# A new order of the attention step, Q and K through the score banks, and 24 leading products on PE

## The chip, the cores and the metric

The kernel runs on one core of a Trainium2 chip. The metric is device time in microseconds (us) of one execution, less is better. The kernel before takes 1670.7 us, the median of 3 runs (1669.65 to 1671.39).

## What is computed

128 sequences of 128 tokens with 256 features: a cross-attention with 16 heads, an additive bias for every head, query and key, and low-rank additions to the three projections, then a layernorm and a mixture of 8 experts in which each token goes to one.

```python
def attention(q, ctx, bias):               # q = layernorm(x); lora(z, W, b, A, B) = z W^T + b + 2 (z A^T) B^T
    qh, kh, vh = lora(q, "q"), lora(ctx, "k"), lora(ctx, "v")        # 16 heads of 16
    scores = einsum('bqhd,bkhd->bhqk', qh * 16 ** -0.5, kh) + bias   # bias: [128, 16, 128, 128] f32
    return einsum('bhqk,bkhd->bqhd', softmax(scores), vh)

x = x + tanh(g_xattn) * attention(layernorm(x), ctx, bias)
idx = argmax(softmax(z @ Wg + bg)) ; z = layernorm(x)
x = x + tanh(g_ffn) * (gelu(z @ W1[idx] + b1[idx]) @ W2[idx] + b2[idx])
```

## The kernel before, in words

Each of the five engines has its own program; semaphores join them and every engine keeps strictly to the order that is written. There are three stages: a setup (weights loaded by 21 transfers, low-rank products L432 to L436, small DVE work), the attention loop, and the expert stage with 72 tiles of 256 tokens. The change touches the first two.

The attention loop is a software pipeline by hand (`run_steps`, L87). Step k works on several sequences at once; `seq(i, k, lag)` names sequence k - lag. A `cur` (lag 0) sequence gets its scores in this step; `prev` (lag 1) is transposed and exponentiated; `fin` (lag 2) is multiplied by V and normalised; `old` (lag 3) has its second layernorm; `gate` (lag 4) gets its expert logits; `nxt` (lag -4) is prepared.

In one step of the kernel before PE does, in this order: `scores` (L451, all four score banks `b_s[0..3]`), the transposes `turn` 0 and 1 (L464), the product with V called PV here (L490, into bank `b_x`), the transposes of the second normalised row block (L502, into `b_x2`, which is `b_s[1]`), the transposes of the attention output OT (L515), logits (L519) and, in every fourth step, slot positions (L523, L524), all three into `b_o`, then the transposes of the next x and ctx (L536, L539, into `b_x`), `turn` 2 and 3, the V projection (L551, L553, into `b_v`, which is `b_s[0]`), and alternately the Q projection (L559) or the K projection (L569) for a pair of sequences, both into `b_x`.

ACT does `probs` (L658, exponentials of a turned quarter), two `normalise` (L651), and the copies out of PSUM: OT (L674), x2T (L679), XT (L687), V (L695), QT (L631), KT (L642).

DVE adds the bias to each score quarter (`add_bias`, L778, four per step, frees a score bank by `s_used`), takes row maxima (L784), then waits for `o_ready` and works on the output bank: L863, L867, L871, L878, with the statistics of the coming layernorms (L792, L795, L801) and at the end L893, which makes `ve`. POOL takes `ve` to the power -1/2 into `rs` (L396), after its two `subtract_max` (L380). DVE makes `shift` from `rs` (L850) one step later, and ACT's `normalise` needs `shift`. In every fourth step DVE begins with `pick_experts` (L806 to L822), in the step behind it with `list_slots`.

Of the kernel before, what the change touches and what calls it, by code (L numbers as in the profile page):

```python
# [98 lines left out]
def flamingo_block(nc, x, ctx_in, bias, g_xattn, g_ffn, wqT, bq, aq, bqT, wkT, bk, ak, bkT, wvT, bv, av, bvT,  # L99
                   wg, bg, w1, w2, b2, consts, row_consts, ids_const, out):  # L100
    ctx = ExitStack()
    with ctx:
# [3 lines left out]
        def sem(name):  # L106
            return ctx.enter_context(nc.semaphore(name))
# [87 lines left out]
        b_v, b_x2 = b_s[0], b_s[1]  # L195
# [5 lines left out]
        s_set = sem("s_set")  # L201
# [33 lines left out]
        SETUP_DMAS = 21  # L235
        SETUP_OPS = 15
# [192 lines left out]
        def _(pe):  # L429
            mm = nc.tensor.matmul  # L430
            pe.wait_ge(s_set, 16 * SETUP_DMAS)
# [34 lines left out]

            def step(i, k):
                nxt, late, cur, prev, fin, old, gate = (seq(i, k, lag) for lag in (-4, -2, 0, 1, 2, 3, 4))
                was_nxt, was_late, was_gate, was_grp = (seq(i, k, lag) for lag in (-3, -1, 5, 6))
                if cur:  # L470
                    pe.wait_ge(v_evac, nxt.n() if nxt else N)
                    if gate:
                        pe.wait_ge(x2t_evac, gate.n(1, 1))
                    scores(cur)
                if prev:
                    turn(prev, 0)
                    turn(prev, 1)

                if was_nxt and was_nxt.slot(2) == 1:
                    pe.wait_ge(q_evac, was_nxt.per(2, 1, 1))  # L480
                if was_late and was_late.slot(2) == 0:
                    pe.wait_ge(k_evac, was_late.per(2, 1, 1))
                if fin:
                    pe.wait_ge(pt_ready, fin.n(4, 4))
                    if fin.reached(1):
                        pe.wait_ge(ot_evac, fin.n())
                    pe.wait_ge(xt_evac, nxt.n() if nxt else N)
                    for h in range(HEADS):
                        j = h % 4
                        ins = mm(b_x[CELL * j:CELL * j + CELL, P * (h // 4):P * (h // 4) + P],  # L490
                                 V[:, fin.slot(8), h, :], PT[:, fin.slot(2), P * h:P * h + P],
                                 start=True, stop=True, tile_position=(0, CELL * j))
                    ins.then_inc(ot_ready, 1)
                if old:
                    pe.wait_ge(xn2_ok, old.n(1, 1))
                    if cur:
                        pe.wait_ge(s_used, cur.n(4, 2))
                    else:
                        pe.wait_ge(s_used, 4 * N)
                        pe.wait_ge(x2t_evac, old.n())  # L500
                    for c in range(KC):
                        ins = nc.tensor.transpose(b_x2[:, c * P:c * P + P],  # L502
                                                  xn2[:, old.slot(8), c * P:c * P + P], ident)
                    ins.then_inc(x2t_ready, 1)

                ins = None
                grp = seq(i, k, 5)
                if old:
                    pe.wait_ge(x2_ok, old.n())
                elif was_gate:  # L510
                    pe.wait_ge(l_ok, was_gate.n(1, 1))
# [13 lines left out]
                if ins:  # L525
                    ins.then_inc(o_ready, 1)
                if nxt:
                    pair, tok = nxt.k // 2 % 2, P * nxt.slot(2)
                    pe.wait_ge(xn_ok, nxt.n(1, 1))
                    pe.wait_ge(ctx_inn[nxt.slot(4)], nxt.per(4, 16, 16))  # L530
                    if nxt.reached(1):
                        pe.wait_ge(xt_evac, nxt.n())
                    if fin:
                        pe.wait_ge(ot_evac, fin.n(1, 1))
                    for c in range(KC):
                        nc.tensor.transpose(b_x[:, c * P:c * P + P],  # L536
                                            xn[:, nxt.slot(2), c * P:c * P + P], ident)
                    for c in range(KC):
                        ins = nc.tensor.transpose(b_x[:, (KC + c) * P:(KC + c) * P + P],  # L539
                                                  ctx_sb[:, nxt.slot(4), c * P:c * P + P], ident)  # L540
                    ins.then_inc(xt_ready, 1)
                if prev:
                    turn(prev, 2)
                    turn(prev, 3)
                if nxt:
                    pe.wait_ge(xt_evac, nxt.n(1, 1))
                    if cur:
                        pe.wait_ge(s_used, cur.n(4, 1))
                    elif nxt.reached(1):
                        pe.wait_ge(v_evac, nxt.n())  # L550
                    mm(b_v[:, 0:HID], top3[:], bv_rows[:], start=True, stop=False)  # L551
                    for c in range(KC):
                        ins = mm(b_v[:, 0:HID], XT[:, pair, KC + c, tok:tok + P], W["v"][:, c, :],  # L553
                                 start=False, stop=(c == KC - 1))
                    ins.then_inc(v_ready, 1)
                if nxt and nxt.slot(2) == 1:
                    for o in range(KC):
                        for c in range(KC):
                            ins = mm(b_x[:, 256 * o:256 * o + 256], W["q"][:, c, o * P:o * P + P],  # L559
                                     XT[:, pair, c, :], start=(c == 0), stop=(c == KC - 1))  # L560
                    ins.then_inc(q_ready, 1)
                if late and late.slot(2) == 0:
                    pair = late.k // 2 % 2
                    pe.wait_ge(xt_evac, nxt.n(1, 1) if nxt else N)
                    if fin:
                        pe.wait_ge(ot_evac, fin.n(1, 1))
                    for o in range(KC):
                        for c in range(KC):
                            ins = mm(b_x[:, 256 * o:256 * o + 256], W["k"][:, c, o * P:o * P + P],  # L569
                                     XT[:, pair, KC + c, :], start=(c == 0), stop=(c == KC - 1))  # L570
                    ins.then_inc(k_ready, 1)
# [47 lines left out]
        def _(act):  # L619
# [5 lines left out]
            def queries(t):  # L625
                pair = t.k // 2 % 2
                act.wait_ge(q_ready, t.per(2, 1, 1))
                if t.reached(4):
                    act.wait_ge(s_ready, t.n(4, -8))
                for o in range(KC):  # L630
                    ins = nc.scalar.activation(QT[:, pair, o, :], b_x[:, 256 * o:256 * o + 256],  # L631
                                               ACT.Identity, bias=bq_col[:, o:o + 1])
                ins.then_inc(q_evac, 1)

            def keys(t):
                pair = t.k // 2 % 2
                act.wait_ge(k_ready, t.per(2, 1, 1))
                if t.reached(4):
                    act.wait_ge(s_ready, t.n(4, -8))
                for o in range(KC):  # L640
                    for e in range(2):
                        ins = nc.scalar.activation(  # L642
                            KT[:, pair, o, :, e, :], b_x[:, 256 * o:256 * o + 256].rearrange("p (s k) -> p s k", s=2),
                            ACT.Identity, bias=bk_half[:, e, o:o + 1], scale=half_rows[e])
# [16 lines left out]
            def step(i, k):  # L661
                nxt, late, prev, fin, old = (seq(i, k, lag) for lag in (-4, -2, 1, 2, 3))
                if prev:
                    probs(prev, 0)
                    probs(prev, 1)
# [4 lines left out]
                if fin:  # L670
# [3 lines left out]
                    nc.scalar.copy(OT[:], b_x[:]).then_inc(ot_evac, 1)  # L674
                if old:
# [5 lines left out]
                if nxt:  # L681
                    pair, tok = nxt.k // 2 % 2, P * nxt.slot(2)
                    act.wait_ge(xt_ready, nxt.n(1, 1))
                    if nxt.reached(4):
                        act.wait_ge(q_ready, nxt.per(2, 1, -1))
                        act.wait_ge(k_ready, nxt.per(2, 1, -1))
                    nc.scalar.copy(XT[:, pair, :, tok:tok + P],  # L687
                                   b_x[:].rearrange("p (c t) -> p c t", t=P)).then_inc(xt_evac, 1)
                if prev:
                    probs(prev, 2)  # L690
                if nxt:
                    act.wait_ge(v_ready, nxt.n(1, 1))
                    if nxt.reached(8):
                        act.wait_ge(ot_ready, nxt.n(1, -7))
                    nc.scalar.copy(V[:, nxt.slot(8), :, 0:D],  # L695
                                   b_v[:, 0:HID].rearrange("p (h d) -> p h d", d=D)).then_inc(v_evac, 1)
                if prev:
                    probs(prev, 3)
                if nxt and nxt.slot(2) == 1:
                    queries(nxt.minus(1))  # L700
                if late and late.slot(2) == 0:
                    keys(late)
# [25 lines left out]
        def _(dve):  # L728

# [106 lines left out]
            def step(i, k):  # L836
# [7 lines left out]
                if cur:  # L844
                    add_bias(cur, 0)
# [6 lines left out]
                if cur:  # L852
                    add_bias(cur, 1)
# [162 lines left out]
```

## Time and profile before

| what | value |
|---|---|
| median of 3 runs | 1670.7 us |
| time of the profiled execution | 1668.51 us |
| its span, first to last instruction | 1666.6 us |
| PE, busy share of the span | 87% |
| DVE | 64% |
| POOL | 57% |
| ACT | 53% |
| mean share of the 16 DMA engines (hardware and software queue) | 61% |
| first scores / end of the attention stage / span | 57.7 / about 1300 / 1666.6 us |

The times of the rows are microseconds from the start of the span. In a timeline row the first number is the start, the second the duration of a group of like instructions that follow each other, "x8" their number, and the bracket says how long the engine was idle before them and what ended that.

### The profile page before, as it was taken

The numbers are of one execution on the slowest core, as the hardware profiler recorded it, in microseconds if no ns is written. First come the engines' busy times: TensorE is split into PE (matmuls) and PEld (weight loads), VectorE is DVE, ScalarE is ACT, GpSimd is POOL, SyncE is SP. The second block draws the span as 40 slices with busy tenths as digits, with TensorE's granted clock in tenths as the row PEclk, the third lists the DMA queues.
The fourth block names the chain that finished last, engine by engine and source line by source line (L and its number), as shares of the span: only waits on it lengthen the run. The fifth ranks groups of instructions, "written<-read, shape, count | busy, mean of one in ns | idle before, by whom it ended". The sixth has DMA issues, their size and how long they took to land.

```text
span 1666.6 us, 43159 instructions
## 1 busy us (share of the span) xinstructions
PE 1450.7 (87%) x13374; PEld 1166.7 (70%) x13374; DVE 1061.8 (64%) x2734; ACT 887.9 (53%) x1883; POOL 942.9 (57%) x671
## 2 busy tenths in 40 slices
PE   3789999989989989989998998998997589999886
PEld 2577777777777777777777777777776468777775
DVE  2477787787788788778778778778877311111111
ACT  1466666666666666666666666666664123333231
POOL 2345555555555555556555555555555356666667
PEclk9999999999999999999999999999999699999998
DMA  4355655555555555555555555555552499999994
GB/s 140 85 164 150 178 163 154 171 170 153 166 175 152 163 174 156 160 175 157 157 174 163 157 168 168 155 167 171 154 166 66 139 249 253 242 226 229 230 221 93
DMA packets 383026, 281.53 MB, mean 169 GB/s; under 512 B 21599, under 2 KB 349691, under 8 KB 382972
## 3 DMA queue, kind: packets, MB, share of 16 engines
q1 hardware_dynamic: 356092, 246.22, 50.8%
q0 software_dynamic: 26880, 34.64, 10.5%
q8 instruction: 29, 0.48, 0.1%
q14 instruction: 25, 0.20, 0.0%
HBM read 226.86 MB, written 56.00 MB: 170 GB/s over the span
## 4 chain that ended last, share of the span: by engine, by line
PE 51%; ACT 18%; DMA 15%; issue 10%; DVE 2%; SPq 1%; POOL 1%; ACTq 1%; POOLq 0%; DVEq 0%
DMA out<-og,ids 14%; PE bank L464 9%; PE bank L553 7%; PE bank L569 7%; PE bank L559 7%; ACT KT L642 5%; PE bank L515 5%; PE bank L451 4%; ACT OT L674 4%; ACT x2n L651 3%; ACT xn L651 3%; PE bank L519 3%; ACT PT L658 2%; PE bank L536 2%; PE bank L598 2%
## 5 line engine op out<-in xcount | busy, mean ns | idle before, releaser
L380 POOL TENSOR_TENSOR sc<-sc,negmax 128x1024 f32<-128x1024 f32 x256 | 484.4, 1892 | 435.6 <-DVE negmax L784 435.6
L778 DVE TENSOR_TENSOR sc<-bank,sc 128x512 f32<-128x512 f32 x512 | 337.6, 684 | 195.2 <-PE bank L451 192.4
L658 ACT ACTIVATE PT<-bank 128x512 f32<-128x512 f32 x512 | 293.3, 603 | 59.7 <-PE bank L464 59.7
L784 DVE TENSOR_REDUCE negmax<-sc 128x8 f32<-128x1024 f32 x256 | 312.3, 1220 | 17.0
L420 POOL DMA_INDIRECT out<-og,ids x144 | 223.5, 1552 | 132.3 <-issue 112.0
L464 PE MATMUL bank<-cst,sc 128*128 128x128 f32 x2048 | 273.6, 277 | 0.7 <-ACT PT L658 0.7
L464 PEld LDWEIGHTS bank<-cst,sc 128*128 128x128 f32 x2048 | 226.6, 142 | 43.1 <-issue 41.8
L943 DVE TENSOR_SCALAR og<-bank,tg 128x512 f32<-128x512 f32 x72 | 54.0, 750 | 276.1 <-DMA out<-og,ids 240.5
L687 ACT COPY XT<-bank 128x512 f32<-128x512 f32 x128 | 75.0, 586 | 183.8 <-PE bank L539 183.8
L396 POOL TENSOR_TENSOR rs<-ve,cst 128x2 f32<-128x2 f32 (+1 forms) x135 | 94.8, 703 | 119.4 <-DVE ve L893 98.9
L642 ACT ACTIVATE KT<-bank,bk_half,cst 128x256 f32<-128x256 f32 x256 | 123.7, 564 | 56.5 <-PE bank L569 56.5
L405 POOL DMA_INDIRECT rows_dram<-x2n,slot_i x128 | 133.5, 1043 | 33.2 <-issue 28.9
L451 PE MATMUL bank<-KT,QT 32*128 32x256 f32 x2048 | 146.7, 400 | 0.0
L612 PE MATMUL bank<-sc,hT 128*128 128x256 f32 x576 | 144.4, 380 | 0.0
L598 PE MATMUL bank<-xgT,w_sb 128*128 128x256 f32 x576 | 140.0, 387 | 4.5 <-issue 2.8
L490 PE MATMUL bank<-PT,V 128*32 128x128 f32 x4096 | 139.2, 277 | 0.7 <-ACT PT L658 0.7
L515 PE MATMUL bank<-cst,OT 128*128 128x128 f32 x512 | 82.4, 284 | 64.1 <-ACT OT L674 63.6
L553 PE MATMUL bank<-wv,XT 128*128 128x256 f32 x512 | 134.6, 386 | 0.0
L712 ACT COPY xgT<-bank 128x512 f32<-128x512 f32 x72 | 42.2, 586 | 158.0 <-PE bank L587 158.0
L451 PEld LDWEIGHTS bank<-KT,QT 32*128 32x128 f32 x2048 | 92.5, 184 | 45.0 <-issue 42.2
L559 PE MATMUL bank<-XT,wq 128*128 128x256 f32 x512 | 123.0, 384 | 0.0
L569 PE MATMUL bank<-XT,wk 128*128 128x256 f32 x512 | 122.4, 382 | 0.0
(120 smaller groups left out, 2196.7 us busy)
## 6 DMA issues: line engine op xcount, KB each, us to landing
sc<-in_bias SPq DMA_DIRECT2D x256, 512.0 KB, 5.1
xg<-rows_dram SPq DMA_DIRECT2D x72, 272.0 KB, 4.0
w_sb<-in_w SPq DMA_DIRECT2D x72, 257.0 KB, 4.1
sc<-in_w SPq DMA_DIRECT2D x72, 256.0 KB
ctx_sb<-in_ctx_in SPq DMA_DIRECT2D x128, 128.0 KB, 5.3
x_sb<-in_x SPq DMA_DIRECT2D x128, 128.0 KB, 2.1
out<-x SPq DMA_DIRECT2D x128, 128.0 KB, 1.7
rows_dram<-vacant SPq DMA_DIRECT2D x9, 272.0 KB, 3.6
```

Source lines behind the costliest of these rows:

```text
L380: nc.gpsimd.tensor_tensor(s, s, m, ALU.add).then_inc(sub_ok, 1)
L420: nc.gpsimd.indirect_dma_start(out_rows, bass.IndirectOffsetOnAxis(ap=ids[:, t.slot(8), a:a + 1], axis=0), og[:, t.slot(2), a, :], None, b ...
L451: ins = mm(b_s[j][:, 2 * P * c:2 * P * c + 2 * P], QT[rows, pair, c, P * sq:P * sq + P], KT[rows, pair, c, sq].rearrange("p e k -> p (e k) ...
L464: ins = nc.tensor.transpose(b_t[q % 2][:, P * h:P * h + P], sc[:, t.slot(4), o:o + P], ident)
L553: ins = mm(b_v[:, 0:HID], XT[:, pair, KC + c, tok:tok + P], W["v"][:, c, :], start=False, stop=(c == KC - 1))
L559: ins = mm(b_x[:, 256 * o:256 * o + 256], W["q"][:, c, o * P:o * P + P], XT[:, pair, c, :], start=(c == 0), stop=(c == KC - 1))
L569: ins = mm(b_x[:, 256 * o:256 * o + 256], W["k"][:, c, o * P:o * P + P], XT[:, pair, KC + c, :], start=(c == 0), stop=(c == KC - 1))
L598: ins = mm(bank[2 + t.slot(2)][:, FT * o:FT * o + FT], w1_sb[:, t.slot(4), c * HID + o * P:c * HID + o * P + P], xgT[:, t.slot(2), c, :], ...
L642: ins = nc.scalar.activation(KT[:, pair, o, :, e, :], b_x[:, 256 * o:256 * o + 256].rearrange("p (s k) -> p s k", s=2), ACT.Identity, bias ...
L658: nc.scalar.activation(PT[:, t.slot(2), 512 * q:512 * q + 512], b_t[q % 2][:], ACT.Exp).then_inc(pt_ready, 1)
L778: nc.vector.tensor_tensor(s, b_s[q][:], s, ALU.add).then_inc(s_used, 1)
L784: nc.vector.tensor_reduce(negmax[:, t.slot(2), 8 * h:8 * h + 8], sc[:, t.slot(4), 1024 * h:1024 * h + 1024].rearrange("p (h k) -> p h k", ...
```

## The change

The PE, ACT and DVE programs of the attention step are put in another order, Q and K get their own lags and other banks, and PE's program starts with 24 products.

- PE: scores, PV, turn 0 and 1, then Q (sequence k+2, even steps) or K (sequence k+1, odd steps) into `b_s[0]` and `b_s[1]` behind a wait for two add_bias of this step, turn 2 and 3, OT, logits and positions, V of the sequence of lag -3 into `b_s[2]`, the x2n transposes into `b_s[3]`, and last the x and ctx transposes of `nxt`.
- ACT: both `normalise`, OT, probs 0 and 1, QT or KT (each half as soon as its own product is there), probs 2 and 3, V, x2T, XT.
- DVE: `shift` (L850) stands ahead of the first `add_bias`.
- Setup: DVE clears `xgT`, and PE multiplies a 128x128 part of it by itself 24 times ahead of its wait for the weights.

```diff
-        b_v, b_x2 = b_s[0], b_s[1]
+        b_v, b_x2 = b_s[2], b_s[3]
+            pe.wait_ge(s_warm, 1)
+            for n in range(WARM):
+                mm(bank[7][:, 0:P], xgT[:, 0, 0, 0:P], xgT[:, 0, 0, 0:P], start=True, stop=True)
             pe.wait_ge(s_set, 16 * SETUP_DMAS)
...
+            def project(w, t, first, ready):
+                pe.wait_ge(xt_evac, t.n(1, 2))
+                for o in range(KC):
+                    for c in range(KC):
+                        ins = mm(b_s[o][:, 0:2 * P], W[w][:, c, o * P:o * P + P],
+                                 XT[:, t.k // 2 % 2, first + c, :], start=(c == 0), stop=(c == KC - 1))
+                    ins.then_inc(ready, 1)
...
+                if prev:
+                    turn(prev, 0)
+                    turn(prev, 1)
+                if cur and (qry or ky):
+                    pe.wait_ge(s_used, cur.n(4, 2))
+                if qry and qry.slot(2) == 0:
+                    if qry.reached(2):
+                        pe.wait_ge(k_evac, qry.per(2))
+                    project("q", qry, 0, q_ready)
+                if ky and ky.slot(2) == 0:
+                    pe.wait_ge(q_evac, ky.per(2, 1, 1))
+                    project("k", ky, KC, k_ready)
+                if prev:
+                    turn(prev, 2)
+                    turn(prev, 3)
...
+                if val:
+                    pair, tok = val.k // 2 % 2, P * val.slot(2)
+                    pe.wait_ge(xt_evac, val.n(1, 1))
+                    if cur:
+                        pe.wait_ge(s_used, cur.n(4, 3))
...
+                if old:
+                    pe.wait_ge(xn2_ok, old.n(1, 1))
+                    if cur:
+                        pe.wait_ge(s_used, cur.n(4, 4))
...
-                if cur:
-                    add_bias(cur, 0)
                 norms = norms_at(i, k - 1)
                 if norms:
                     a, b = norms
...
                 if cur:
+                    add_bias(cur, 0)
                     add_bias(cur, 1)
```

## Rows read from the trace of the kernel before

**Rows 1.** The stages view: busy us of each engine, steps 6 to 123.
```profile
108.96:1237.75 1128.79, 1025.44 (x10764) 825.32 (x10763) 894.47 (x2307) 712.85 (x1520) 644.24 (x464) 1.00 0.56 164
```
**Rows 2.** The timeline of PE: the scores of sequences 0, 4 and 124.
```profile
57.73 1.15 PE L451 MATMUL bank<-KT,QT 32*128 32x256 f32 x16
...
89.97 1.15 PE L451 MATMUL bank<-KT,QT 32*128 32x256 f32 x16
...
1247.33 1.15 PE L451 MATMUL bank<-KT,QT 32*128 32x256 f32 x16
```
**Rows 3.** The timeline of PE, one step.
```profile
842.42 1.15 PE L451 MATMUL bank<-KT,QT 32*128 32x256 f32 x16
...
844.52 1.08 PE L490 MATMUL bank<-PT,V 128*32 128x128 f32 x32
845.89 0.43 PE L502 MATMUL bank<-cst,x2n 128*128 128x128 f32 x2 [0.29 <-ACT x2n L651]
846.77 0.66 PE L515 MATMUL bank<-cst,OT 128*128 128x128 f32 x4 [0.45 <-ACT OT L674]
847.27 0.51 PE L519 MATMUL bank<-wg_sb,x2T 128*128 128x8 f32 x4
847.63 0.42 PE L536 MATMUL bank<-cst,xn 128*128 128x128 f32 x2
...
848.10 1.04 PE L464 MATMUL bank<-cst,sc 128*128 128x128 f32 x8
...
850.00 1.89 PE L569 MATMUL bank<-XT,wk 128*128 128x256 f32 x8
851.82 1.15 PE L451 MATMUL bank<-KT,QT 32*128 32x256 f32 x16
```
**Rows 4.** The waits view of steps 6 to 123: total, times, longest us.
```profile
DVE sc L778 <- PE bank L451: 168.9, 105, 2.2
...
DVE lmax L806 <- issue: 4.1, 12, 0.4
```
**Rows 5.** The timeline of DVE in the same step.
```profile
843.58 0.69 DVE L778 TENSOR_TENSOR sc<-bank,sc 128x512 f32<-128x512 f32 x1 [2.24 <-PE bank L451]
...
848.65 0.16 DVE L863 TENSOR_TENSOR L<-bank,bg_all 128x8 f32<-128x8 f32 x1
...
850.89 0.17 DVE L893 TENSOR_SCALAR ve<-mv 128x2 f32<-128x2 f32 x1
```
**Rows 6.** The timeline of POOL, same step: the power behind L893.
```profile
851.14 0.72 POOL L396 TENSOR_TENSOR rs<-ve,cst 128x2 f32<-128x2 f32 x1 [0.43 <-DVE ve L893]
```
**Rows 7.** The timeline of DVE, a step that begins with pick_experts.
```profile
860.37 0.18 DVE L806 TENSOR_REDUCE lmax<-L 128x4 f32<-128x32 f32 x1
...
862.62 0.69 DVE L778 TENSOR_TENSOR sc<-bank,sc 128x512 f32<-128x512 f32 x1 [0.21 <-PE bank L451]
```
**Rows 8.** The timeline of PE, the positions of such a step and what follows.
```profile
828.02 0.39 PE L523 MATMUL bank<-OH,cst 128*128 128x32 f32 x2
...
828.47 0.42 PE L536 MATMUL bank<-cst,xn 128*128 128x128 f32 x2
```
**Rows 9.** The timeline of ACT, the copy of x2T.
```profile
846.61 0.39 ACT L679 COPY x2T<-bank 128x256 f32<-128x256 f32 x1
```
**Rows 10.** The timeline ahead of the first scores.
```profile
11.51 2.07 PE L434 MATMUL bank<-bq,aq 8*128 8x256 f32 x4 [11.51 <-DMA cnt<-in_bg]
...
34.51 0.60 ACT L651 ACTIVATE xn<-x_sb,shift,rs 128x256 f32<-128x256 f32 x1
...
38.85 3.62 PE L559 MATMUL bank<-XT,wq 128*128 128x256 f32 x8
```
**Rows 11.** The stages view, 10 to 20 us (columns as in rows 1).
```profile
10.00:20.00 10.00, 5.48 (x12) 3.82 (x12) 2.75 (x10) 0.20 (x1) 0.00 (x0) 1.00 0.01 0
```
**Rows 12.** The timeline of DVE: the first bias addition of sequences 126 and 127.
```profile
1263.63 0.69 DVE L778 TENSOR_TENSOR sc<-bank,sc 128x512 f32<-128x512 f32 x1
...
1270.87 0.69 DVE L778 TENSOR_TENSOR sc<-bank,sc 128x512 f32<-128x512 f32 x1
```

More of the change, by code:

```diff
@@ L198, in flamingo_block @@
         pos_ps = o_ps[:, 1:HEADS:4, D + 4:D + 4 + EXPERTS]
-        s_set = sem("s_set")
+        s_set, s_warm = sem("s_set"), sem("s_warm")
         s_bv, bv_in, s_b2, b2_out = sem("s_bv"), sem("bv_in"), sem("s_b2"), sem("b2_out")
@@ L235, in flamingo_block @@
         SETUP_DMAS = 21
+        WARM = 24
         SETUP_OPS = 15
@@ L465, in turn @@
                 ins.then_inc(tr_ready, 1)
+            def project(w, t, first, ready):
[5 more added lines that the diff above has]
+                    ins.then_inc(ready, 1)
             def step(i, k):
-                nxt, late, cur, prev, fin, old, gate = (seq(i, k, lag) for lag in (-4, -2, 0, 1, 2, 3, 4))
-                was_nxt, was_late, was_gate, was_grp = (seq(i, k, lag) for lag in (-3, -1, 5, 6))
+                nxt, val, qry, ky, cur, prev, fin, old, gate, grp = (
+                    seq(i, k, lag) for lag in (-4, -3, -2, -1, 0, 1, 2, 3, 4, 5))
+                was_gate = seq(i, k, 5)
                 if cur:
-                    pe.wait_ge(v_evac, nxt.n() if nxt else N)
+                    pe.wait_ge(v_evac, val.n() if val else N)
                     if gate:
@@ L474, in step @@
                     scores(cur)
[L475 to L482, printed above, removed]
                 if fin:
                     pe.wait_ge(pt_ready, fin.n(4, 4))
-                    if fin.reached(1):
-                        pe.wait_ge(ot_evac, fin.n())
                     pe.wait_ge(xt_evac, nxt.n() if nxt else N)
@@ L493, in step @@
                     ins.then_inc(ot_ready, 1)
-                if old:
-                    pe.wait_ge(xn2_ok, old.n(1, 1))
-                    if cur:
[L497 to L509, printed above, removed]
+                if prev:
[13 more added lines that the diff above has]
+                    turn(prev, 3)
+                ins = None
+                if old:
+                    pe.wait_ge(x2_ok, old.n(1, 1))
                 elif was_gate:
@@ L526, in step @@
                     ins.then_inc(o_ready, 1)
+                if val:
[3 more added lines that the diff above has]
+                        pe.wait_ge(s_used, cur.n(4, 3))
+                    elif val.reached(1):
+                        pe.wait_ge(v_evac, val.n())
+                    mm(b_v[:, 0:HID], top3[:], bv_rows[:], start=True, stop=False)
+                    for c in range(KC):
+                        ins = mm(b_v[:, 0:HID], XT[:, pair, KC + c, tok:tok + P], W["v"][:, c, :],
+                                 start=False, stop=(c == KC - 1))
+                    ins.then_inc(v_ready, 1)
+                if old:
+                    pe.wait_ge(xn2_ok, old.n(1, 1))
+                    if cur:
+                        pe.wait_ge(s_used, cur.n(4, 4))
+                    else:
+                        pe.wait_ge(s_used, 4 * N)
+                        pe.wait_ge(x2t_evac, old.n())
+                    for c in range(KC):
+                        ins = nc.tensor.transpose(b_x2[:, c * P:c * P + P],
+                                                  xn2[:, old.slot(8), c * P:c * P + P], ident)
+                    ins.then_inc(x2t_ready, 1)
                 if nxt:
-                    pair, tok = nxt.k // 2 % 2, P * nxt.slot(2)
                     pe.wait_ge(xn_ok, nxt.n(1, 1))
@@ L541, in step @@
                     ins.then_inc(xt_ready, 1)
[L542 to L571, printed above, removed]
             run_steps(pe, FIRST, LAST, U, LOOP, step)
@@ L626, in queries @@
                 pair = t.k // 2 % 2
-                act.wait_ge(q_ready, t.per(2, 1, 1))
                 if t.reached(4):
@@ L630, in queries @@
                 for o in range(KC):
-                    ins = nc.scalar.activation(QT[:, pair, o, :], b_x[:, 256 * o:256 * o + 256],
+                    act.wait_ge(q_ready, t.per(2, KC, o + 1))
+                    ins = nc.scalar.activation(QT[:, pair, o, :], b_s[o][:, 0:2 * P],
                                                ACT.Identity, bias=bq_col[:, o:o + 1])
@@ L636, in keys @@
                 pair = t.k // 2 % 2
-                act.wait_ge(k_ready, t.per(2, 1, 1))
                 if t.reached(4):
@@ L640, in keys @@
                 for o in range(KC):
+                    act.wait_ge(k_ready, t.per(2, KC, o + 1))
                     for e in range(2):
                         ins = nc.scalar.activation(
-                            KT[:, pair, o, :, e, :], b_x[:, 256 * o:256 * o + 256].rearrange("p (s k) -> p s k", s=2),
+                            KT[:, pair, o, :, e, :], b_s[o][:, 0:2 * P].rearrange("p (s k) -> p s k", s=2),
                             ACT.Identity, bias=bk_half[:, e, o:o + 1], scale=half_rows[e])
@@ L661, in step @@
             def step(i, k):
[L662 to L665, printed above, removed]
+                nxt, val, qry, ky, prev, fin, old = (seq(i, k, lag) for lag in (-4, -3, -2, -1, 1, 2, 3))
                 if old:
@@ L674, in step @@
                     nc.scalar.copy(OT[:], b_x[:]).then_inc(ot_evac, 1)
+                if prev:
+                    probs(prev, 0)
+                    probs(prev, 1)
+                if qry and qry.slot(2) == 0:
+                    queries(qry)
+                if ky and ky.slot(2) == 0:
+                    keys(ky)
+                if prev:
+                    probs(prev, 2)
+                    probs(prev, 3)
+                if val:
+                    act.wait_ge(v_ready, val.n(1, 1))
+                    if val.reached(8):
+                        act.wait_ge(ot_ready, val.n(1, -7))
+                    nc.scalar.copy(V[:, val.slot(8), :, 0:D],
+                                   b_v[:, 0:HID].rearrange("p (h d) -> p h d", d=D)).then_inc(v_evac, 1)
                 if old:
@@ L684, in step @@
                     if nxt.reached(4):
-                        act.wait_ge(q_ready, nxt.per(2, 1, -1))
-                        act.wait_ge(k_ready, nxt.per(2, 1, -1))
+                        act.wait_ge(k_ready, nxt.per(2, KC, -KC))
                     nc.scalar.copy(XT[:, pair, :, tok:tok + P],
                                    b_x[:].rearrange("p (c t) -> p c t", t=P)).then_inc(xt_evac, 1)
[L689 to L702, printed above, removed]
             run_steps(act, FIRST, LAST, U, LOOP, step)
@@ L728, in _ @@
         def _(dve):
+            nc.vector.memset(xgT[:], 0.0).then_inc(s_warm, 1)
             dve.wait_ge(s_set, 16 * SETUP_DMAS)
@@ L843, in step @@
                     list_slots(was_grp)
-                if cur:
-                    add_bias(cur, 0)
                 norms = norms_at(i, k - 1)
```

## Prediction

> **What bounds the kernel now.** I read the stages view first: from step 6 to step 123 PE is busy 1025 of 1129 us, DVE 894, ACT 713, POOL 644, the DMA engines 56%, at full granted clock [rows 1]. PE is the fullest, so the next view is its timeline. The starts of the scores give the length of a step: from sequence 4 to 124 it is (1247.33 - 89.97) / 120 = 9.645 us [rows 2]. Inside one step PE stands twice, 0.29 us for the second normalised block and 0.45 us for OT [rows 3]; both are ACT copies whose input PE made a moment before. By starts, which leave out the overlap, the work of a step is: scores with turn 0 and 1 2.10, PV about 1.05 (its 1.08), L502 0.23 (half of four transposes, 0.47), L515 0.50 and L519 0.36, x and ctx 0.47, turn 2 and 3 with V 1.90, K 1.82 [rows 3]. That is 8.43 us of 9.40; the rest, 0.97 us, is the two waits with the draining that goes with them. DVE meanwhile waits 168.9 us in those 117 steps for scores, 1.44 us a step [rows 4]. So PE's order bounds the loop, and DVE follows by a little over a microsecond.
>
> **PE's part.** No product is added or removed in the loop. What moves: PV goes ahead of the turns, so ACT copies OT under 0.9 us of turns, 1.74 us of Q or K and 0.9 us of turns; that wait goes (0.45 us). The x2n transposes stand near the end of the step, and `normalise` for them at its head, several us earlier; that wait goes too (0.29 us). What is late next on PE is the border of two steps: the next scores need x2T copied. L502 takes 0.43 us [rows 3], the copy 0.39 [rows 9], handovers some 0.1 together (an estimate from those rows), so scores can start 0.92 us after L502 starts, while PE has only 0.23 + 0.47 us to do there, and some 0.08 for the change of tiling: a gap of about 0.14 us. PE alone would therefore need 8.43 + 0.14 = 8.57 us, less about 0.1 since three changes of tiling stand in the order in place of four: 8.5, and the pick step 0.45 more for positions [rows 8]. That would be 8.6 us a step.
>
> The trace shows no scores directly followed by PV. The nearest rows are scores followed by turns and turns followed by PV; I bound the pair between 0.1 us less and 0.35 us more than the sum above. The Trainium skill, TensorEngine Tiling (Array Packing), Key Properties, says that changing the tiling mode drains TensorE; by that rule alone the new order has one drain less, which would be a gain of about 0.1 us a step and no loss. The sum holds without it.
>
> **DVE's part, which I take for the new bound.** DVE is strictly in order, and `shift` now stands ahead of the first add. It waits for POOL's `rs`, which waits for DVE's last operation of the step before. Queued behind that wait are all four adds, both maxima and the output work; PE's Q or K waits for the second add, and all of PE's step stands behind that. The loop, from add to add [rows 5]: add to L863 is 5.07 us, less 0.07 for the shift that leaves it, 5.00; L863 to L893 2.24; from L893 to POOL's start 0.25 and 0.72 for the power [rows 6]; then 0.05 and 0.08 until the add. Together 8.34 us, against 9.40 now, where the same wait was hidden under the wait for scores.
>
> L863 waits for `o_ready` on PE. Two adds (2 x 0.69, less overlap, 1.33 [rows 5]) free the banks; then Q or K 1.74, turns 0.91, L515 0.50 and L519 until its end 0.51 make 3.66 [rows 3], plus handovers 0.05: 5.04 us after the add. DVE itself is there after 5.00. So both chains run side by side with 0.04 us between: DVE-PE-DVE. In the pick step, once in four, pick_experts takes from 860.37 to 862.62, and the add was hardly waiting for PE there [rows 7]; it stands in line with `shift` behind L893, 2.40 us in all against 1.10 for the round trip of `rs`: +1.30. Positions add 0.45 to `o_ready` in that step [rows 8], with the 0.04 above. list_slots and the extra operation cost between 0 (hidden behind `rs`) and 0.5 us; I take 0.25, an estimate. At the head of each loop of 8 steps 0.34 us is lost (4.1 / 12 [rows 4]), 0.04 a step. Four steps: 4 x 8.34 + 1.30 + 0.25 + 3 x 0.04 + 0.49 = 35.5, or 8.88 a step, and 0.04: **8.92 us**. That is above PE's 8.6, so PE will stand for some 0.3 us a step, in the pick step over a microsecond ahead of Q or K. 120 steps x (9.645 - 8.92) = **87 us** less.
>
> ACT has the room: 713 us in 117 steps is 6.1 us a step [rows 1]. Its QT or KT work is hidden behind turns, OT and V, and costs up to 1 us a step if it comes late. POOL's 5.5 us are hidden too. On SP nothing is moved; the transfers run at 56% [rows 1] and would go to 61%; the output store and what is queued behind it on SP wait for x2, about 0.8 us later in a step, hidden by a bias that is loaded three steps ahead.
>
> **The ends of the loop.** Ahead of the first scores, steps are a single chain: the second xn starts at 34.51 because ACT first copied V [rows 10], and Q takes 3.62 us in line with the rest. The new order lets xn, the transposes and XT of one sequence run while V, Q or K of an earlier one is on PE. Going through the four steps by these durations I get the first scores at 44.5 to 47.5 us, against 57.73 [rows 2]; I take 12 us less. The four short steps behind it give 1 us. At the end, the last three adds followed DVE's own work at once (7.24 us from 126 to 127, no wait [rows 12]); there the round trip of `rs`, about 0.9 us, is now exposed three times, plus a little in the drain: +3 us.
>
> **The 24 products.** PE waits until 11.51 us for the weights; then 12 passes of 256 columns take 5.48 us busy [rows 10, 11]. Passes of Q stand 0.43 us apart at 38.85 (3.62 for 8) [rows 10], those of K 0.23 (1.82 for 8) [rows 3]. 
>
> **Sum:** 87 + 12 + 1 + 2 - 3 = 99 us. Against the profiled execution: 1668.5 - 99 = 1569.5; the median of the runs lies 2.2 us above that execution, so about 1572 us. The expert stage is not touched.
>
> **The rivals.**
> - *PE is still the bound.* Were `rs` back sooner, or the order tighter than I read it, the step would be PE's 8.6: 120 x 1.045 + 12 = 137 less, **1533 us**. For it: PE is the fullest engine [rows 1]. Against it: the round trip [rows 5, 6] contains no slack. 7%.
> - *PE and DVE couple worse than the sum.* Drains between scores and PV, late KT copies, or `s_used` arriving late each go once through the loop DVE-PE-DVE, where only 0.04 us is free. Price 0.2 to 0.5 us a step, 24 to 60 us: **1596 to 1632 us**. For it: the 0.04. Against it: all terms are from rows at full clock. 23%.
> - *The moved `shift` makes it slower.* The wait for `rs` comes ahead of the first add and PE's Q or K waits behind it; if that wait were longer than the PE work between scores and Q or K (2 us) by more than the 0.73 us that the order gains, all gain is gone. The 1.10 us round trip would have to be 1.8 us or more in every step, for instance because POOL reaches L396 late behind its two L380: 2 us a step instead gives 9.85 a step, 120 x 0.2 = 24 slower, less 12: **1683 us**. Against it: POOL waited for `ve`, not `ve` for POOL [rows 6]. 4%.
> - *The reordering hides nothing* because an ACT copy takes the place of those removed, 0.7 us at the border in place of 0.14: about 9.6 us a step, only the head of the loop gains, **1658 us**. 3%.
>
> **How the numbers follow.** My forecast has 63%: its own bounds are 8.8 to 9.1 us a step and 8 to 13 us at the head, 1555 to 1598. The range that holds 8 in 10 takes in half of the first rival and most of the second: 1545 to 1616. A measurement of this kernel can tell about 0.2% (3.3 us) from no change. Faster 0.95, same 0.01, slower 0.04.
>
> **What would show it.** In the profile of the changed kernel: scores 8.9 us apart, with every fourth step about 1.5 us longer; DVE idle ahead of `shift` with POOL's `rs` as releaser, and hardly any wait for scores; PE idle ahead of Q or K with the second add as releaser; no wait ahead of L515's and L502's successors; first scores near 45 us; the low-rank products at 0.23 us a pass. I am wrong if PE waits longest at the border of steps, if DVE still waits for scores, or if the first scores are later than 50 us.

## The result and the profile after

The changed kernel takes **1594.9 us** (median of 4, 1591.2 to 1599.0) against 1670.2, a ratio of 0.9558 (95% interval 0.9518 to 0.9599): 4.4% faster. The forecast was 1572 (1545 to 1616). The gain is 75 us where 99 were forecast. One term of the sum, 2 us for the 24 products, was mis-sized by much more: without them the kernel took 21 to 120 us longer, which only an experiment showed.

The profiled execution took 1598.95 us, its span is 1596.9. The timeline of PE, the scores of sequences 0, 4 and 124 (to be read against [rows 2]):

```profile
43.94 1.15 PE L455 MATMUL bank<-KT,QT 32*128 32x256 f32 x16
...
74.90 1.15 PE L455 MATMUL bank<-KT,QT 32*128 32x256 f32 x16
...
1166.66 1.15 PE L455 MATMUL bank<-KT,QT 32*128 32x256 f32 x16
```

The first scores come 13.8 us sooner, the four short steps behind them give 1.3, and 120 steps of (1166.66 - 74.90) / 120 = 9.098 us in place of 9.645 give 65.6. From the scores of sequence 124 to the first expert tile it is 5.9 us more than before (74.17 against 68.27), and the untouched expert stage behind it is 5.1 us longer in this execution (356.1 against 351.0; in a second profile of the changed kernel it is 350.8). 13.8 + 1.3 + 65.6 - 5.9 - 5.1 = 69.7, the difference of the two spans.

The waits view from 200 to 1100 us (total, times, longest us) shows the new bound. These are the waits of DVE and PE that bear on it; ACT and POOL wait longer in total, behind DVE and PE:

```profile
DVE shift L844 <- POOL rs L397: 53.1, 74, 0.9
...
PE bank L475 <- DVE sc L774: 39.2, 41, 2.0
...
DVE L L858 <- PE bank L530: 13.2, 24, 2.1
...
DVE x L873 <- issue: 4.9, 10, 0.8
```

The wait of DVE for scores, 168.9 us before [rows 4], is not in the list any more (in the same window of the kernel before it was 131.3). DVE now stands ahead of `shift` for POOL's `rs`, PE stands ahead of Q or K for the second bias addition, and DVE for the positions of the pick step. One step of it, in the timelines of DVE, POOL and PE:

```profile
638.26 0.17 DVE L888 TENSOR_SCALAR ve<-mv 128x2 f32<-128x2 f32 x1
...
639.34 0.16 DVE L844 SCALAR_TENSOR_TENSOR shift<-mv,rs 128x2 f32<-128x2 f32 x1 [0.91 <-POOL rs L397]
639.44 1.29 DVE L774 TENSOR_TENSOR sc<-bank,sc 128x512 f32<-128x512 f32 x2
```
```profile
638.59 0.72 POOL L397 TENSOR_TENSOR rs<-ve,cst 128x2 f32<-128x2 f32 x1 [0.80 <-DVE ve L888]
```
```profile
637.74 1.15 PE L455 MATMUL bank<-KT,QT 32*128 32x256 f32 x16
638.82 1.08 PE L493 MATMUL bank<-PT,V 128*32 128x128 f32 x32
639.83 1.09 PE L468 MATMUL bank<-cst,sc 128*128 128x128 f32 x8
640.78 1.99 PE L475 MATMUL bank<-XT,wq 128*128 128x256 f32 x8
...
646.21 1.15 PE L455 MATMUL bank<-KT,QT 32*128 32x256 f32 x16
```

The two additions end at 640.73 and Q starts at 640.78. The turns in front of it ended their issue at about the same time: in such a step (8.47 us) both chains arrive together. In the pick step they don't:

```profile
619.18 0.19 DVE L802 TENSOR_REDUCE lmax<-L 128x4 f32<-128x32 f32 x1 [0.34 <-issue]
...
621.55 1.29 DVE L774 TENSOR_TENSOR sc<-bank,sc 128x512 f32<-128x512 f32 x2
```
```profile
622.90 1.99 PE L475 MATMUL bank<-XT,wq 128*128 128x256 f32 x8 [1.33 <-DVE sc L774]
```

The DVE timeline from 100 to 1160 us, taken apart as in the prediction and averaged over 29 groups of four steps (us; in brackets what was forecast, where 2.57 is the 2.40 of the pick step and half of the 0.34 us that is lost once in 8 steps at the head of a round):

| step, from its first addition | add to L858 | L858 to ve | ve to next add | sum |
|---|---|---|---|---|
| behind pick_experts | 5.61 (5.49) | 2.43 (2.49) | 1.20 (1.10) | 9.25 (9.08) |
| the next | 5.17 (5.04) | 2.27 (2.24) | 1.17 (1.10) | 8.61 (8.38) |
| the next | 5.03 (5.04) | 2.32 (2.24) | 1.13 (1.10) | 8.48 (8.38) |
| the one that ends with pick_experts | 5.17 (5.04) | 2.43 (2.24) | 2.58 (2.57) | 10.18 (9.85) |

The 5.61 is 5.50 in 27 of 29 steps and 7.17 in the two in which PE's clock had fallen (see the last section).

### The profile page after: what moved, and what is told of

Its sections match the earlier page's. It is cut to its first block, busy times and chain, and to the rows that moved or that the text cites. A ratio compares the mean times of both kernels' runs of the same rounds, so it can differ in the third digit from the quotient of the medians.

```text
span 1596.9 us, 43185 instructions
## 1 busy us (share of the span) xinstructions
PE 1431.2 (90%) x13422; PEld 1194.2 (75%) x13422; DVE 1077.9 (68%) x2735; ACT 899.5 (56%) x1883; POOL 942.8 (59%) x671
## 4 chain that ended last, share of the span: by engine, by line
PE 36%; DMA 25%; DVE 16%; issue 12%; POOL 6%; SPq 3%; DVEq 1%; POOLq 0%; ACT 0%; ACTq 0%
DMA out<-og,ids 16%; PE bank L475 10%; DMA rows_dram<-x2n,slot_i 8%; PE bank L468 8%; POOL sc L381 4%; PE bank L455 3%; DVE sc L774 3%; PE bank L493 3%; PE bank L542 3%; PE bank L521 2%; PE bank L525 2%; DVE st L791 2%; DVE x L873 2%; DVE CNT L818 1%; DVE mv L797 1%
## 5 line engine op out<-in xcount | busy, mean ns | idle before, releaser
L774 DVE TENSOR_TENSOR sc<-bank,sc 128x512 f32<-128x512 f32 x512 | 328.5, 683 | 3.8 <-PE bank L455 2.5
L656 ACT ACTIVATE PT<-bank 128x512 f32<-128x512 f32 x512 | 277.9, 597 | 2.9 <-PE bank L468 2.9
L468 PEld LDWEIGHTS bank<-cst,sc 128*128 128x128 f32 x2048 | 231.7, 142 | 46.2 <-issue 32.7
L649 ACT ACTIVATE x2n<-x,shift,rs 128x256 f32<-128x256 f32 x128 | 76.9, 601 | 226.7 <-DVE shift L844 193.1
L475 PE MATMUL bank<-XT,wq 128*128 128x256 f32 x512 | 130.3, 398 | 41.7 <-DVE sc L774 41.0
L475 PEld LDWEIGHTS bank<-XT,wq 128*128 128x128 f32 x512 | 93.5, 193 | 63.0 <-DVE sc L774 49.1
L493 PEld LDWEIGHTS bank<-PT,V 128*32 128x32 f32 x4096 | 104.6, 110 | 42.4 <-issue 42.3
L475 PE MATMUL bank<-XT,wk 128*128 128x256 f32 x512 | 125.6, 388 | 11.2 <-DVE sc L774 8.4
L455 PEld LDWEIGHTS bank<-KT,QT 32*128 32x128 f32 x2048 | 98.4, 184 | 47.8 <-ACT V L684 38.3
```

Source lines behind the costliest of these rows:

```text
L455: ins = mm(b_s[j][:, 2 * P * c:2 * P * c + 2 * P], QT[rows, pair, c, P * sq:P * sq + P], KT[rows, pair, c, sq].rearrange("p e k -> p (e k) ...
L468: ins = nc.tensor.transpose(b_t[q % 2][:, P * h:P * h + P], sc[:, t.slot(4), o:o + P], ident)
L475: ins = mm(b_s[o][:, 0:2 * P], W[w][:, c, o * P:o * P + P], XT[:, t.k // 2 % 2, first + c, :], start=(c == 0), stop=(c == KC - 1))
L656: nc.scalar.activation(PT[:, t.slot(2), 512 * q:512 * q + 512], b_t[q % 2][:], ACT.Exp).then_inc(pt_ready, 1)
L774: nc.vector.tensor_tensor(s, b_s[q][:], s, ALU.add).then_inc(s_used, 1)
```

## The experiments

The theories: **A**, DVE with the round trip of `rs` sets the step, closely followed by PE (A'); **B**, PE alone; **C**, the scatter of x2n rows holds DVE up at the x2 addition, which explains the gaps in the third column of the table. All times are medians. Differences are taken from the 1592.0 us of the changed kernel's second timing; it stood beside the first four runs, while the others stood beside the kernel before alone, and their ratios to that one are given.

**The changed kernel again.**

> The changed kernel itself, as the yardstick for the other runs beside it: 1592 to 1599 us, scores 9.1 us apart, against 1670 for the kernel before.

1592.0 us (1590.5 to 1593.7), ratio 0.9545 (0.9519 to 0.9571), 9.103 us a step.

**The round trip made longer.**

```diff
+ nc.gpsimd.tensor_tensor(spare[:, a:b, 0], ve[:, a:b, 0], minus_half.broadcast_to([P, b - a]), ALU.pow)
  nc.gpsimd.tensor_tensor(rs[:, a:b, 0], ve[:, a:b, 0], minus_half.broadcast_to([P, b - a]), ALU.pow).then_inc(rs_ok, 1)
```

> The changed kernel with one more power of the same size on POOL ahead of the one that makes rs, 0.72 us; nothing reads its result. Theory A (the round trip of rs stands in the loop DVE-POOL-DVE-PE): three steps of four are longer by about 0.7 us, the one that pick_experts hides is not, so 0.5 us a step and 60 to 65 us in all, about 1657 us. Theory B (PE alone bounds the step now, and DVE has slack): under 10 us.

1652.3 us, 60 more. The timelines of POOL and DVE:

```profile
640.47 0.72 POOL L398 TENSOR_TENSOR spare<-ve,cst 128x2 f32<-128x2 f32 x1 [0.56 <-DVE ve L891]
641.17 0.68 POOL L400 TENSOR_TENSOR rs<-ve,cst 128x2 f32<-128x2 f32 x1
```
```profile
641.88 0.16 DVE L847 SCALAR_TENSOR_TENSOR shift<-mv,rs 128x2 f32<-128x2 f32 x1 [1.57 <-POOL rs L400]
```

By kind of step, add to add: 9.79, 9.26, 9.12 and 10.13. The three steps that wait for `rs` are 0.54 to 0.66 us longer than in the table, the one that pick_experts covers is not longer. That is A, and B, PE alone, falls.

**The scatter's wait on another engine.**

```diff
 # DVE, ahead of the x2 addition
-dve.wait_ge(x2_out[done.slot(8)], done.per(8, 16))
 # ACT, ahead of normalise of x2, one step later
+if old.reached(8):
+    act.wait_ge(x2_out[old.slot(8)], old.per(8, 16))
```

> The changed kernel, but the wait for the scatter of x2n rows (x2_out) stands on ACT ahead of normalise one step later, no longer on DVE ahead of the x2 addition. Theory C (the scatter, which is issued one step before and takes 5.7 us to land, holds DVE up by 0.067 us a step on average, over 0.2 us in a dozen steps): 5 to 10 us less, and no gap over 0.61 us ahead of the x2 addition. Rival (those gaps are hidden by PE anyway): within 2 us.

1580.8 us, 11 less, ratio 0.9473 (0.9444 to 0.9503), 9.01 us a step; L858 to ve falls to 2.39, 2.25, 2.25 and 2.25 us. C holds, a little above its range. Inside the loop of the changed kernel (100 to 1160 us) the scatter takes 4.2 to 6.7 us to land (median 5.7); it is issued behind `rs` of one step, and the x2 addition of the next now comes some 6.1 us later, where before it came 7.1. So only the slow landings are late, and DVE stood ahead of 28 of 116 such additions. One of those gaps, in a pick step of the changed kernel:

```profile
910.35 0.42 DVE L873 TENSOR_TENSOR x<-bank,x_sb 128x256 f32<-128x256 f32 x1 [0.59 <-issue]
```

**shift behind the first addition again.**

```diff
+if cur: add_bias(cur, 0)
 if norms: ... shift ...
-if cur: add_bias(cur, 0)
```

> The changed kernel with shift behind the first bias addition again, all else as changed. Theory A in its strict form (DVE with the round trip alone sets the time): 0.6 us of the round trip is hidden in three steps of four, 0.45 us a step, 54 us less, about 1541. Theory A' (DVE's loop of 8.4 us and PE's own work of 8.4 us stand side by side, so taking one away leaves the other): 0.1 to 0.2 us a step, 12 to 25 us less, 1570 to 1583. If moving shift ahead was what made the order work: slower.

1573.9 us, 18 less, ratio 0.944 (0.9415 to 0.9464): A', not the strict form. Of the three steps without pick_experts most are now 8.34 us, where they were 8.46 to 8.96, and DVE waits 15.3 us for scores again: 8.34 us is the length of PE's own work, as combo below shows. The scatter's gap grew (L858 to ve 2.48 us on average in place of 2.36).

**The same line in the kernel before.**

> The kernel before with one line moved: shift ahead of the first bias addition, as in the changed kernel. In the kernel before, DVE's first addition starts 2.1 to 2.5 us after its last operation of the step before, and the round trip of rs takes 1.2 us of that. If the round trip costs only where PE no longer makes DVE wait: steps unchanged, 0 to 4 us more in all, from the last three steps (0.7 us each). If moving shift is a loss by itself: 0.5 us a step, 60 us more.

1670.2 us beside 1668.8, ratio 1.0004 (0.9988 to 1.0021); 9.645 us a step, as before. The moved line costs nothing as long as PE makes DVE wait, and 18 us once it doesn't.

**Both single edits.**

> The changed kernel with shift behind the first addition and the scatter's wait on ACT: both single edits together. They gained 18 and 11 us alone. If the scatter's wait grew when shift moved (the gap ahead of the x2 addition took 0.18 us a step there against 0.07 here), together they gain more than their sum: 30 to 38 us less than the changed kernel, 1554 to 1562. If PE's own work is reached first: 20 to 25 us less.

1557.2 us, ratio 0.9341 (0.9311 to 0.9371), 8.82 us a step. 18 and 11 alone, 34 together (0.0204 x 1669). The difference of 34 from their sum is within the intervals, but the step lengths of the profiles point the same way: 0.128 and 0.093 us less alone, 0.282 together. With `shift` moved, the scatter's gap had grown (2.48 us above); with both edits L858 to ve is 2.28.

**pick_experts behind the second addition, by itself.**

```diff
-if grp and grp.slot(4) == 3: pick_experts(grp)
 if norms: ... shift ...
 if cur: add_bias(cur, 0); add_bias(cur, 1)
+if grp and grp.slot(4) == 3: pick_experts(grp)
 if cur: row_max(cur, 0)
```

> The changed kernel with pick_experts behind the second bias addition, all else as changed. If PE's wait ahead of Q in that step (1.3 to 2 us, once in four steps) is what sets the time: 0.3 us a step, 36 us less. If DVE's loop sets it: pick_experts no longer fills the wait for rs, and the same 2.3 us now stand between additions and maxima; within 8 us of the changed kernel, either sign.

1592.9 us, ratio 0.9552 (0.9539 to 0.9566), the same as the changed kernel, 9.103 us a step. The waits view from 200 to 1100 us:

```profile
DVE shift L842 <- POOL rs L397: 74.9, 99, 0.9
...
PE bank L475 <- DVE sc L774: 36.9, 25, 1.8
```

PE's wait ahead of Q in the pick step is gone (1.31 us on average in the changed kernel, 0.06 here), but PE now waits 1.64 us in the step behind it, where it waited 0.25, because the work of pick_experts stands ahead of DVE's maxima and so delays the next additions. And DVE waits for `rs` in all steps, 99 times in place of 74, since pick_experts no longer fills that wait. The wait was moved, not removed.

**All of them, with pick_experts behind the second addition.**

> As the run before, and pick_experts behind the second addition, so that PE's Q or K does not wait for it in one step of four. If PE's wait there (1.3 us, once in four steps, 0.33 us a step) is what is left: 20 to 40 us less than the run before, 1520 to 1540. If DVE's total work bounds these steps (the 2.3 us of pick_experts now stand ahead of the maxima, and no longer fill the wait for rs): within 10 us of the run before.

1542.5 us (1540.6 to 1548.5), ratio 0.9260 (0.9235 to 0.9285). 15 us less than the two single edits together: between the two forecasts. The timeline of PE:

```profile
613.53 1.15 PE L455 MATMUL bank<-KT,QT 32*128 32x256 f32 x16
...
621.87 1.15 PE L455 MATMUL bank<-KT,QT 32*128 32x256 f32 x16
...
630.21 1.15 PE L455 MATMUL bank<-KT,QT 32*128 32x256 f32 x16
```

8.34 us from scores to scores with no wait of PE ahead of Q or K, twice in a row: PE's work by itself, for which I had put 8.5.

**list_slots there too.**

> The best kernel so far (1542.5 us), with list_slots behind the second addition too. There PE's step takes 8.34 us in three of four and is 9.47 in the step of list_slots, where Q or K waits 0.9 us. With that wait gone and DVE 0.45 us ahead in two steps: 0.1 to 0.2 us a step, 12 to 25 us less, 1518 to 1531. If DVE's total work is the limit: the same within 3 us.

1539.4 us (1537.1 to 1541.3), ratio **0.9233** (0.9220 to 0.9247), the best of all; 3 us less than the run before, at the edge of what the intervals tell apart and far from the 12 to 25 of the first forecast. From scores to scores the steps take 8.79, 9.27, 8.34 and 8.34 to 8.58 us. Only in the second of them does PE still wait ahead of K, 0.7 us. The others are PE's own work (8.34, and 0.45 more with the positions), so DVE's work, the expectation's other reading, sets one step in four at most.

**Without the 24 products.**

```diff
-nc.vector.memset(xgT[:], 0.0).then_inc(s_warm, 1)
-pe.wait_ge(s_warm, 1)
-for n in range(WARM):
-    mm(bank[7][:, 0:P], xgT[:, 0, 0, 0:P], xgT[:, 0, 0, 0:P], start=True, stop=True)
```

> The changed kernel without the 24 products and without the clearing of xgT. From the trace of the changed kernel the first two of six low-rank products run at 0.23 us a pass and the last ones at 0.43: the setup should get 1.2 us longer (first DVE operation behind the products at 17.1 us in place of 15.9), the first scores come at 45.1 in place of 43.9 us. If the products have a later effect on the clock too, the passes of Q and V between 30 and 40 us change their length.

One execution, 1613.1 us. The setup is 1.2 us longer, as expected (first DVE operation behind the low-rank products at 17.09 us against 15.94), but the first scores come at 42.45 us, not at the 45.1 that I expected. The waits view of PE and the queue of instruction loads:

```profile
PE bank L452 <- issue: 16.0, 6, 4.2
```
```profile
q8 instruction: 47, 0.77, 0.2%
```

The changed kernel has 29 packets on that queue.

> The same kernel without the 24 products, timed against others this time. The single look before took 1613 us, and its trace has what no other has: PE stood 16.0 us in 6 places ahead of scores, waiting for nothing that the profile shows, and the queue of instruction loads moved 47 packets in place of 29. If that belongs to the kernel (its program lies elsewhere by 96 instructions): 1603 to 1615 us in all executions and again more than 40 packets. If it was a single disturbance: 1590 to 1597.

1639.2, 1656.6, 1710.4 and 1712.5 us, in executions beside which the kernel before stayed within 1665.6 to 1669.0 and pick_later, which has the products, within 1590.5 to 1593.6. The two faster ones give a ratio of 0.9885 (0.9831 to 0.9939) to the kernel before. The profile is that of the fastest; the two slowest left none. Its waits view, and its timeline at the head of one round of the loop:

```profile
PE bank L452 <- issue: 35.3, 12, 4.0
```
```profile
502.61 0.89 PE L452 MATMUL bank<-KT,QT 32*128 32x256 f32 x6 [3.37 <-issue]
507.55 1.86 PE L452 MATMUL bank<-KT,QT 32*128 32x256 f32 x10 [4.04 <-issue]
509.33 1.93 PE L490 MATMUL bank<-PT,V 128*32 128x128 f32 x32
511.20 1.97 PE L465 MATMUL bank<-cst,sc 128*128 128x128 f32 x8
```

And its transfers from 500 to 600 us, a stretch in which the changed kernel loads no instructions at all:

```profile
q8 instruction: 11, 0.18, 0.9%
```

At the start of a round of the loop (8 steps) PE stands twice for 2.9 to 4 us, ahead of the scores and in the middle of them, and instructions are loaded at the same time (packets of that queue start at 498, 505 and 509 us, around the lines above). Behind each pair of stalls PE runs at half its clock: the granted clock is 0.50 from 503 to 513 us, and PV takes 1.93 us in place of 1.08. There are five such pairs in this profile, from 254 to 591 us; the half clock behind them lasts 6.8 to 10.2 us each, 41 us together. Its span is 46 us longer than that of the changed kernel's second profile, of which the stalls are 35.3; the half clock is the nearest explanation of the rest (an estimate, from the durations above).

Every kernel here loads instructions during the first rounds of the loop, and without such stalls: the last of these loads is at 280 us in the kernel before and at 238 to 257 us in the new orders with the products. Without the products the loads go on to 411 us in the first profile and to 655 us in this one, and then end by themselves.

**96 empty instructions in their place.**

```diff
-for n in range(WARM):
-    mm(bank[7][:, 0:P], xgT[:, 0, 0, 0:P], xgT[:, 0, 0, 0:P], start=True, stop=True)
+for n in range(4 * WARM):
+    pe.nop(nofuse=True)
```

> The changed kernel with 96 empty PE instructions in place of the 24 products (each product is 4 instructions), and without the clearing. If what the products give is the place of the program behind them: 29 packets, no stalls, within 3 us of the changed kernel. If it is their work (a raised clock): like the kernel without them, wherever that one comes out. The low-rank products run slow in both, 1.2 us of setup.

1613.3, 1658.1, 1686.8 and 1708.2 us; in its profile, that of the 1658.1 us:

```profile
PE bank L454 <- issue: 49.9, 16, 4.5
```

The queue of instruction loads has 92 packets here, the last one in the loop at 823 us. The number of instructions ahead of the loop is not what helps, at least not to within the one wait for `s_warm` that this kernel has less. The faster low-rank products can hardly be it either: they are over at 15.8 us, and worth 1.2 us. Both of these kernels also lack the clearing of `xgT` and PE's wait for it, so no run tells these from the products themselves; "the products" below stands for all three.

## Why the prediction was right, and where it was off

- **The bound moves to DVE with the round trip of `rs`, PE close behind: right.** Predicted 8.92 us a step, measured 9.098. slow_rs and shift_second show both halves of the claim, the loop and the nearness of PE. One reading was loose: of the two waits of PE that go, only OT is a copy of what PE had just made. `normalise` (L651) takes its input from DVE and stood behind two exponentials, which had waited 0.74 us for PE's transposes; its wait of 0.29 us went all the same.
- **The size of the step: 0.18 us short, 21 of the 24 us that are missing.** Four terms, each under 0.1 us a step. L858 to ve was taken as 2.24 (2.49 behind pick_experts); the scatter, which the sum left out altogether, adds 0.07 us there (wait_on_act: 0.09 a step and 11 us in all). In the steps with K, add to L858 is 5.19 for 5.04, since K starts 0.22 us behind the second addition and not 0.05; Q starts 0.06 behind it. Ve to add is 0.03 to 0.10 us more, since POOL starts 0.25 to 0.33 us behind L888 and I took the lower end from one row [rows 6]. The two steps with a fallen clock add 0.03.
- **pick_experts: right to 0.01 us** (2.58 against 2.57, the 0.34 us at the head of a round included). pick_later shows that moving it behind the second addition gains nothing.
- **PE's own step: 8.34 measured, 8.5 put.** The pair of scores and PV, bounded from -0.1 to +0.35, came out at the lower end: PV starts 1.08 us behind the scores, as the turns did, and from scores to Q it is 3.02 us in combo (613.53 to 616.55) where the sum had 2.10 + 1.05 = 3.15. The Trainium skill, TensorEngine Tiling (Array Packing), Key Properties, has every change of tiling mode drain the engine. The traces agree in sign, one change less and 0.13 us shorter, but no run isolates it.
- **The head of the loop: 12 + 2 us put, 13.8 measured in one execution.** In the other profiles of kernels with the new order the first scores stand at 40.8 to 44.1 us, with or without the products, so the head is known to some 3 us only. Most of that is the clock: in after_again it is back at its full level at 33.4 us and Q takes 1.99 us, in the changed kernel's first profile it is back at 40.0 us and Q takes 3.78. The low-rank products gave 1.2, not 2. PE had stood from 9.4 to 11.5 us, the granted clock fell to 0.50 at 12.7, and their last passes ran at the slow length again:

```profile
1.96 7.48 PE L434 MATMUL bank<-xgT 128*128 128x128 f32 x48 [1.96 <-DVE xgT L725]
11.50 1.13 PE L438 MATMUL bank<-bq,aq 8*128 8x256 f32 x4 [2.06 <-DMA cnt<-in_bg]
...
13.92 1.91 PE L438 MATMUL bank<-bv,av 8*128 8x256 f32 x4
```

- **The end: +3 put, +5.9 measured** (+8.0 in after_again, 76.24 us from the scores of sequence 124 to the first expert tile against 68.27). before_shift, in which only `shift` moved, has 2.0 of it (70.29), which fits the exposed round trips. The rest is not shown by a run; it may be the two more ACT exponentials that now stand ahead of the last positions in the drain.
- **The 24 products: the term that failed.** "So nothing more comes of it" priced them at 2 us, the rest of the order at 97. In the new order the three fastest executions without them took 21, 47 and 65 us more than the 1592.0 us with them, the slowest 120 more: single executions lie between 56 us less (1613) and 46 us more (1712) than the kernel before beside them. So the order without the products, priced at 97 us, gave 56 at best, and that the total still came within the range owes something to luck. What the products do is shown by its effect (instruction loads end at about 250 us, no stalls of 2.9 to 4.5 us at the head of a round, no half clock behind them), not by its cause. The kernel before has the same rounds, no products and no such stalls, so it is the new order without the products that brings them. Why 96 empty instructions don't do the same is open; untried are other numbers of products, the clearing and the wait without products, and products without the wait ahead of them.
- **The slower rival** had its mechanism right, a wait for `rs` ahead of everything: at 1.1 us it costs 18 us of the gain, and before_shift shows that it costs nothing where PE is late. Its threshold was too low. slow_rs, with 1.8 us, still takes 9.55 us a step against 9.645 and 0.9903 (0.9867 to 0.9939) of the time before, where I had expected the gain of the loop to be gone; one step in four hides the wait behind pick_experts, which the rival left out.

## What to carry to other kernels

When an order of work takes away the wait that covered another engine's round trip, price the whole ring of engines anew, and look for every wait that had a microsecond to spare. Here the loop over `rs` and PE's own work came within 0.12 us of each other (8.46 and 8.34 us a step), and the scatter's landing (5.7 us in the median) within 0.4 us of its deadline (6.1). PE's largest wait in the waits view (39.2 us, for the second addition) could not be had by moving one piece of DVE's work: it turned up one step later. Two small edits that gain 18 and 11 us alone gained 34 together, so it pays to try the second-ranked wait together with the first. A part of a change that looks like a trifle (24 products at the head) has to be taken out, and timed in several executions, before it is priced.

## What the hardware showed that I had not expected

- PE can stand in the middle of a loop that has run many rounds while instructions are being loaded: twice 2.9 to 4.5 us a round, 16 to 50 us in a profile, with 47, 74 and 92 packets on the queue of instruction loads in place of 29. The loads ended by themselves at 411, 655 and 823 us. Single executions of one program lay up to 99 us apart (1613 to 1712); in the three that left a profile, with spans of 1611, 1637 and 1656 us, the stalls take 16, 35 and 50 us.
- PE's clock, at its full level through the whole loop before, now drops at times in a pick step, where PE waits longest. The stages view (rightmost three: granted clock, DMA share, GB/s), and PE's timeline in it:

```profile
910.00:920.00 10.00, 7.67 (x77) 6.22 (x75) 7.99 (x21) 5.02 (x11) 4.56 (x5) 0.86 0.53 158
```
```profile
915.86 2.46 PE L475 MATMUL bank<-XT,wq 128*128 128x256 f32 x8 [1.97 <-DVE sc L774]
...
918.11 1.92 PE L468 MATMUL bank<-cst,sc 128*128 128x128 f32 x8
```

  Eight transposes take 1.92 us there in place of 1.04, the 1.2 GHz level in place of 2.4; the step is 2.3 us longer than its like, 0.6 of it the scatter's gap. It happened twice inside the loop of this profile (at 842 and 917 us), twice in after_again (477 and 1170 us) and three times in shift_second, and never in the loop of combo and combo_b, where PE waits less. By the 7.17 against 5.50 us beside the table it cost 3.3 us in this profile. The Trainium skill, TensorE: Matmul & The Clock Gate, HAM oscillation, says that idle gaps of PE throttle it again. The trace agrees in kind: PE had been idle for 1.94 and 1.97 us a moment before. But an idle time of 1.90 us at 331.6 us was not followed by a fall, so the length of the gap alone does not tell.
